# Attention's last unit: sums on VectorE, early products moved, first expert weights split sooner

## The reference, cut to what matters

```python
# x: (8, 512, 512), ctx: (8, 512, 512); 16 heads of 32; float32 throughout
x = x + attn(layernorm(x), ctx, ctx) @ Wo.T + bo        # softmax attention, every score computed
flat = layernorm(x)                                     # 4096 tokens of 512
logits = flat @ router_weight.T + router_bias           # 8 experts, the best two of each token
gate, up = split(flat @ gate_up_proj[e] + bias)         # per expert: 512 -> 2 x 512
act = (clip(up, -7, 7) + 1) * min(gate, 7) * sigmoid(1.702 * min(gate, 7))
x = x + sum over the token's two experts of softmax weight * (act @ down_proj[e] + bias)
```

## Time and profile before

| | |
|---|---|
| median of 3 runs | 1673.5 us (1672.38 to 1676.56) |
| the profiled execution | 1674.36 us, of it span 1672.6 us |
| PE busy | 1580.5 us, 94% |
| VectorE busy | 1310.3 us, 78% |
| GpSimd busy | 838.9 us, 50% |
| ScalarE busy | 695.8 us, 42% |
| mean granted TensorE clock | 0.983 |

### The profile page before, as it was taken

The page is one execution under the profiler, slowest core; times in us unless marked ns, Lnnn a source line. Parts: engine busy times, 40 slices in busy tenths (PEclk is TensorE's granted clock), DMA queues, the critical chain, the costliest instruction groups (busy, mean ns, idle before and its releaser), DMA issues. The chain is left out here.

```text
span 1672.6 us, 30419 instructions
## 1 busy us (share of the span) xinstructions
PE 1580.5 (94%) x9607; PEld 1160.5 (69%) x9607; DVE 1310.3 (78%) x2477; ACT 695.8 (42%) x1316; POOL 838.9 (50%) x628
## 2 busy tenths in 40 slices
PE   5898999999999999999998799979999999999996
PEld 4555555555555555555553498879999999999995
DVE  4576777878778778787786588878889878888886
ACT  3354544545445446454445243342434334333431
POOL 3355656566666676666678413223333333433333
PEclk9999999999999999999999799989999999999999
DMA  6343433353543444434334814544546345354433
GB/s 222 85 114 85 113 99 105 110 109 90 119 103 107 96 107 105 120 76 115 97 95 71 209 65 156 197 139 136 188 146 191 113 150 187 110 162 148 134 128 107
DMA packets 112246, 209.48 MB, mean 125 GB/s; under 512 B 32400, under 2 KB 33808, under 8 KB 112080
## 3 DMA queue, kind: packets, MB, share of 16 engines
q1 hardware_dynamic: 91248, 144.73, 31.7%
q0 software_dynamic: 20640, 62.49, 12.1%
q10 hardware_dynamic: 192, 0.26, 0.0%
HBM read 204.33 MB, written 37.51 MB: 145 GB/s over the span
## 5 line engine op out<-in xcount | busy, mean ns | idle before, releaser
L872 DVE TENSOR_REDUCE negmax<-max_ps 128x2 f32<-128x1024 f32 x252 | 306.9, 1218 | 140.7 <-PE max_ps L599 136.9
L730 ACT ACTIVATE pt<-work 128x512 f32<-128x512 f32 x512 | 278.0, 596 | 262.6 <-PE work L611 252.4
L1111 POOL TENSOR_TENSOR acc<-acc,pt 128x1024 f32<-128x1024 f32 x128 | 303.8, 2377 | 116.5 <-ACT pt L730 116.4
L1108 POOL TENSOR_TENSOR acc<-pt 128x1024 f32<-128x1024 f32 x64 | 153.4, 2398 | 180.9 <-PE work L631 112.7
L599 PE MATMUL max_ps<-ks,qs 96*128 96x512 f32 x504 | 193.9, 466 | 22.5 <-DVE negmax L872 13.4
L1600 ACT ACTIVATE sig<-gate 128x256 f32<-128x256 f32 x156 | 65.3, 419 | 293.7 <-DVE gate L1660 282.7
L1493 PE MATMUL gu_ps<-xgT_hi,early_wg_hi 128*128 128x256 f32 x640 | 179.8, 281 | 1.5 <-DVE xgT_lo L1652 1.5
L1493 PE MATMUL gu_ps<-xgT_lo,early_wg_hi 128*128 128x256 f32 x640 | 177.9, 278 | 0.0
L1493 PE MATMUL gu_ps<-xgT_hi,early_wg_lo 128*128 128x256 f32 x640 | 177.8, 278 | 0.0
L611 PE MATMUL work<-qs,ks 98*128 98x512 f32 x512 | 168.2, 407 | 6.6 <-DMA qs<-m_lo 3.9
L1493 PE MATMUL gu_ps<-xgT_hi,wg_hi 128*128 128x256 f32 x608 | 170.7, 281 | 0.0
(11 more groups left out here) (303 smaller groups left out, 3678.0 us busy)
## 6 DMA issues: line engine op xcount, KB each, us to landing
early_raw_g<-w_gate_up SPq DMA_DIRECT2D x39, 2048.0 KB
early_raw_d<-w_down SPq DMA_DIRECT2D x20, 1024.0 KB
raw_d<-w_down SPq DMA_DIRECT2D x19, 1024.0 KB
qs<-q_hi SPq DMA_DIRECT2D x252, 64.0 KB
ks<-k_hi SPq DMA_DIRECT2D x252, 64.0 KB
bd<-b_down SPq DMA_DIRECT2D x39, 256.0 KB
x_in<-x SPq DMA_DIRECT2D x36, 256.0 KB, 3.4
ctxT_raw<-ctx_t SPq DMA_DIRECT2D x32, 256.0 KB, 3.5
```

Source lines behind the costliest of these rows:

```text
L730: e.activation(pt[k % 2][:, h, :], in_work("exp", u, k, h)[:, :], ACT.Exp, scale=scale).then_inc(exped.sem, 1)
L872: e.tensor_reduce(negmax[:, u % 2, n:n + 2], pair_of(u, r)[:, :, :], AX.X, ALU.max, negate=True).then_inc(maxed.sem, 1)
L1108: e.tensor_tensor(acc[:, heads, :], pt[0][:, heads, :], pt[1][:, heads, :], ALU.add).then_inc(added.sem, 1)
L1111: e.tensor_tensor(acc[:, heads, :], acc[:, heads, :], pt[k % 2][:, heads, :], ALU.add).then_inc(added.sem, 1)
```

## The change

- The scores and exponentials 2 and 3 of the last key tile of the last unit move from round 0 of step 32 into round 7 of step 31, ahead of the products "out 28 0" and "out 29 0", which move to round 1 of step 32. "out 30 0" and "out 31 0" move to round 2, behind "sum 31".
- The six adds of the last unit are issued by VectorE instead of GpSimd.
- The four parts of "split_early" move from round 7 of step 31 to rounds 3, 4, 5 and 6.
- The load of g moves from step 31, round 2 to step 30, round 4; "whole_tokens" and the load of d to step 31, round 0.
- The eight list scatters of the last group move from step 31, rounds 2 and 3, and step 32, round 1, to step 32, round 3, behind "fetch_early", which moves from round 2 to round 1.

```diff
@@ step
-                if u in units:
+                if u in units and (r or u < units[-1]):
                     at(r, *[("exp", u, j // 2, 2 * (j % 2) + i) for i in range(2)])
...
+                if r == 7 and s == units[-1]:
+                    at(r, ("exp", s, T - 1, 2), ("exp", s, T - 1, 3))
...
-            if s == units[-1]:
-                at(2, ("list", groups[-1], 0))
-                at(3, ("list", groups[-1], 1))
             if s == units[-1] + 1:
-                at(1, ("list", groups[-1], 2), ("list", groups[-1], 3))
+                at(3, *[("list", groups[-1], t) for t in range(T)])
...
+            if s == units[-2]:
+                at(4, ("load_early", "g"))
             if s == units[-1]:
-                at(2, ("load_early", "g"), ("whole_tokens",), ("load_early", "d"))
-                at(7, *[("split_early", k) for k in range(C)])
+                at(0, ("whole_tokens",), ("load_early", "d"))
+                for k in range(C):
+                    at(3 + k, ("split_early", k))
             if s == units[-1] + 1:
                 at(0, ("load_early", "g1"))
-                at(1, ("token_of",))
-                at(2, ("fetch_early", 0), ("fetch_early", 1))
-
-
-            if s == units[-1]:
-                at(7, ("out", tokens[-T], 0), ("out", tokens[-T] + 1, 0))
+                at(1, ("token_of",), ("fetch_early", 0), ("fetch_early", 1))
+
+
             if s == units[-1] + 1:
-                at(1, ("out", tokens[-T] + 2, 0), ("out", tokens[-T] + 3, 0))
+                at(1, ("out", tokens[-T], 0), ("out", tokens[-T] + 1, 0))
+                at(2, ("out", tokens[-T] + 2, 0), ("out", tokens[-T] + 3, 0))
@@ attention_stage (add_weights moved out of on_pool, with e as its first argument)
+        def add_weights(e, u, k, p):
+            heads = slice(2 * p, 2 * p + 2)
+            e.wait_ge(exped.sem, exped[u, k, 2 * p + 1])
+            if k == 1:
+                if u:
+                    e.wait_ge(summed.sem, summed[u - 1])
+                e.tensor_tensor(acc[:, heads, :], pt[0][:, heads, :], pt[1][:, heads, :], ALU.add).then_inc(added.sem, 1)
+            else:
+                e.wait_ge(added.sem, added[u, k - 1, p])
+                e.tensor_tensor(acc[:, heads, :], acc[:, heads, :], pt[k % 2][:, heads, :], ALU.add).then_inc(added.sem, 1)
@@ on_dve
+                elif kind == "add" and what[0] == units[-1]:
+                    add_weights(e, *what)
@@ on_pool
-                elif kind == "add":
-                    add_weights(*what)
+                elif kind == "add" and what[0] < units[-1]:
+                    add_weights(e, *what)
```

More of the change, by code:

```diff
@@ L1100, in add_bo @@
                 e.tensor_tensor(sums_of(n), sums_of(n), bo_rows[:, :], ALU.add).then_inc(bo_added.sem, 1)
[L1102 to L1111, removed]
             e.memset(early["ones_e"][:, :], 1.0).then_inc(s_route, 1)
```

## The result

| | before | after |
|---|---|---|
| median of 10 runs each, taken in turn | 1677.03 us (1672.38 to 1680.57) | 1684.14 us (1679.51 to 1690.31) |
| ratio | | 1.0042, 95% interval 1.0028 to 1.0057 |
| the profiled execution | 1674.36 us | 1680.86 us, span 1679.1 us |

The change makes the kernel slower, by 0.42%, about 7 us. That is more than the 0.3% that the prediction took as its bound for no change. The median of before is 3.5 us above the one that the prediction started from.

A forecast was written before the change was run, and what follows sets the result against it. PE is busy for most of the span; VectorE's chain to the last logits was taken to set the barrier. ln2 28 1.9 us later and a tail of 5.2 instead of 6.4 gave +0.7 on 1673.5: 1674.2 us, range 1669.3 to 1678.0.

The forecast's parts named there:

- Adds and low parts at 1.14 apart, 1.21 long, with no gap, the last ending at 923.2: VectorE from 905.15: ten adds and low parts take 11.4 us; on GpSimd the last add ended at 924.7.
- Rival C: VectorE does not keep up: at 1.88 us each, adds and low parts end at 931; 1679.7 us, chance 0.04.
- sum 31 at 923.3, out 28 1 at 929.6: PE: the sum comes 5.1 us sooner, but only 1.7 us reach the next link, x2 28.
- Twelve indirect DMAs from 924 to 939, rstd 28 at 939.8, ln2 28 at 939.9: GpSimd's block of twelve takes 15.0 us ahead of rstd 28, making ln2 28 1.9 us later.
- Rival A: GpSimd's block is not late: ln2 28 at 936.3, end 2.9 us sooner, 1670.6, or 1668.1 with full clock; chance 0.25.
- ln2 31 at 945.1: Tail: 5.2 us behind ln2 28 instead of 6.4, as a store lands sooner; 0.7 us later than before.
- rival D: It only shuffles: the last store holds ln2 31 again until 944.4; end as before, 1673.5; chance 0.11.
- the 5.9 us behind it and the barrier are unchanged: Block end: the PE, ACT and DVE chain from ln2 31 to the last logits keeps its length; barrier at 951.7.
- rival B: GpSimd's block starves PE: ln2 28 at 940.8, half clock reaches further, 2 us; end 3.6 later, 1677.1; chance 0.12.
- SP and the load of g at nothing: SP's queue: the earlier load and the list reads cost zero; at worst up to 1 us, if the maxima meet it.
- Clock behind the barrier: PE from 951 to 960: unknown; full clock would give back about 2.5 us, more half clock cost 1 to 2.

The follow-up runs named there:

- e6: e3 with the six adds of the last unit back on GpSimd, the splits still early; 1682.28 us beside 1675.18 for the kernel before.
- e2: Kernel before with only the list scatters moved as in the change, to round 3 of step 32 behind the gathers; 1680.73 us beside 1676.11.
- e3: Changed kernel with the list scatters where the kernel before has them; 1674.71 us beside 1676.11 for the kernel before.
- e4: Changed kernel with the list scatters at the very end of the stage, behind the last rstd; 1689.87 us beside 1676.11 for the kernel before.
- e12: Changed kernel with the scatters of tiles 0 and 1 in step 31, only 2 and 3 behind the gathers; 1673.36 us beside 1675.56 for the kernel before.
- e8: Changed kernel with the first list entry behind the gathers, the others each behind one of rstd 28, 29, 30; 1684.51 us beside 1675.18 before.
- e1: Changed kernel with all eight list scatters early, in rounds 2 and 3 of step 31; 1677.3 us beside 1676.11 for the kernel before.
- e9: e5 with three of the four tiles' scatters in step 31 and one ahead of the gathers; 1675.28 us beside 1676.59 for the kernel before.
- e10: e5 with all four tiles' scatters in step 31; 1678.25 us beside 1676.59 for the kernel before.
- e5: e3 with out 28 1 and out 29 1 ahead of out 31 0 on PE; 1673.72 us beside 1675.18 for the kernel before.
- e7: Kernel before with only the six adds of the last unit moved to VectorE; 1674.43 us beside 1675.18.
- e11: e5 run once more, unchanged; 1675.63 us beside 1675.56 for the kernel before.

## Why the prediction was wrong

- *Adds and low parts at 1.14 apart, 1.21 long, with no gap, the last ending at 923.2:* right (1.22, to 923.05). The Trainium skill's rule (SBUF — State Buffer, "Who interferes with whom"), by which a VectorE instruction with two SBUF inputs contends with a GpSimd instruction that reads SBUF, holds here from both sides: 1.22 us with no GpSimd arithmetic beside it, 15.17 us in e6. Rival C falls.
- *sum 31 at 923.3, out 28 1 at 929.6:* 923.19 and 929.44, right. So is the point that only a third of the sum's 5 us reaches the next link.
- *Twelve indirect DMAs from 924 to 939, rstd 28 at 939.8, ln2 28 at 939.9:* 924.15 to 939.2, 940.1 and 940.14, right as a count of issues. Rival A falls with it.
- *ln2 31 at 945.1:* 945.67, 0.6 late. It isn't held by a store, so rival D is out.
- *"the 5.9 us behind it and the barrier are unchanged":* **this step failed**, by 6.1 us in sum, in two terms.
  - The barrier, 4.4 us. I took it to follow the last logits. It waits for GpSimd's DRAIN, which ends 2.66 us behind the landing of the last indirect DMA. I priced a list scatter by what it costs GpSimd to issue, 1.25 us, and asked who waits in its queue. I did not ask when it lands, nor what waits for that. e2 and e3 show that this one part makes the loss (0.27% on the old kernel; none without it), e4 that it does so with nothing in the queue behind it, e12 that half of the scatters fit.
  - The chain behind ln2 31, 1.7 us: 7.6 instead of 5.9. I counted the tail through ln2 31 and so booked 1.2 us as won when ln2 31 no longer waits for a store. The tail runs through ln2 30 and PE's work on the tiles in turn: 8.1 us from ln2 30 to the last logits in both traces, at 1.2 GHz nearly throughout. Nothing was won there, and ln2 30 itself came 0.9 us later for the half clock that set in 2 us sooner. I had said that I expect half clock for the tail again, and priced its coming sooner only inside rival B. In e6 and e12, at half clock from before ln2 30 to the barrier, the two parts again take 5.1 and 8.1 us; in e3, at full clock, 4.2 and 6.2. (In e4, at full clock up to 1 us before the last logits, they took 4.2 and 8.3; what held the second there isn't shown.)
- *Rival B* came nearest, with the slower side and a part of its clock, but its mechanism, the late rstd 28, isn't the one that costs most: e8 and e4 have ln2 28 at 936.0 and are slower than the kernel before all the same, e4 even than after.
- *SP and the load of g at nothing:* no row speaks against it. The maxima and the sums come as before.
- *Clock behind the barrier:* 2.4 GHz is granted again at 964.8, 6.4 us behind the barrier, where it took 8.8 us before. The stage behind is 0.9 us shorter, which may come of it; the traces differ there by up to 2.3 us in any case.

The row that could have told it was in the trace before: GpSimd idle for 7.9 us ahead of its first IOTA behind the barrier, released by POOLq:

```profile
951.04 0.24 POOL L2029 IOTA iota_i<- 128x128 int32 x1 [7.91 <-POOLq L1293]
```

I followed the chain back from the last logits, since they ended 0.8 us ahead of the barrier, and took a near coincidence for the cause.

What stays open: e2 shows 2.2 us between logits and barrier and after 5.2, for one and the same move. With the traces shifted as in the table, its last scatter was issued 0.5 us sooner and its DRAIN ended 3.3 us sooner (954.8, after 958.0), and so did the last landing. Why the landings went faster there isn't shown. A floor of 5.9 to 6.0 us for the DRAIN in e1, e3, e9, e10 and e12 isn't explained either. And in e1, e5, e7, e9, e10 and e12 the clock was halved from about 899 to 906, and it fell before anything that the lists have in another order. In e1, e5, e9, e10 and e12 sum 31 came at about 925 with it. It isn't tied to an edit: e11, the same code as e5, had its half clock from 907 to 910 and sum 31 at 924.0. The marks of e5 and e11 differ by up to 2.3 us, so a difference of that size between two single traces says little; the verdicts go by the medians.

## What to carry to other kernels

Price an indirect DMA twice: by its issue on GpSimd, and by its landing, and ask of both who waits. In these runs the end of a block waited for GpSimd's outstanding indirect DMAs, though no instruction of the block waits for the late scatters' semaphore. So the last of them belong far ahead of a block's end, and few at a time. Before moving anything toward a barrier, look at which engine's DRAIN ends last there and by how little it leads.

## What the runs showed of the hardware

- GpSimd's DRAIN at the end of the block ended 2.66 to 2.67 us behind the last landing of GpSimd's indirect DMAs in nine traces (a scatter's in after, e2, e4 and e8, a gather's in before, e5, e6, e7 and e11), and never sooner than 5.9 us after its own start. It was the last DRAIN to end in before, after, e2, e4 and e8, up to 24.48 us long. SP's, with direct stores out, took 0.12 us.
- A list scatter (128 partitions, four bytes each) took 0.97 us to issue and 8.0 us to land when first in line, the next ones one behind another, about 2.6 us apart on average (after). The Trainium skill, DMA: Bandwidth & Descriptors, section "Anatomy of one DMA — SWDGE (gpsimd) path", puts the fixed cost of a DMA at about 2 us, mostly its completion, and warns that a write to HBM can take surprisingly long. The direction agrees; the 8.0 us are four times that figure.
- Gathers landed 5.3 to 6.7 us after their issue ahead of the scatters (after) and 9.9 to 10.8 us behind four of them (e5).
- Beside the scatters the direct stores issued from 934 on took 12 to 20 us to land (after), against 2.1 us in e4 with none in flight, while the DMA engines showed a share of 1.16 at 47 GB/s.
- A VectorE instruction with two SBUF inputs was not let in between GpSimd's adds: it was held through six of them in a row, 15.17 us (e6), although its record starts 0.15 us before the first.
